# Second attention: where TensorE issues the products of the weighted values, and the order of the score banks

## The reference

```python
qk = jnp.einsum('bhdq,bhdl->bhql', qh, kh) * scale      # qh, kh: 32 sequences, 8 heads, 8 x 256
sm = jax.nn.softmax(qk, axis=-1)
ret = jnp.einsum('bhql,bhdl->bhdq', sm, vh)
return gamma * ret.reshape(B, Dv, Lq)
```

## Time and profile before

| | |
|---|---|
| median of 3 runs | 675.91 us (674.12 to 676.22) |
| the profiled execution's own time | 673.21 us |
| its span, first to last instruction | 671.5 us |
| mean granted TensorE clock | 0.952 of full speed |
| PE busy | 603.9 us, 90% of the span |
| DVE busy | 489.4 us, 73% |
| ACT busy | 404.1 us, 60% |
| POOL busy | 313.0 us, 47% |

### The profile page before, as it was taken

How to read it: one execution, slowest core, us unless ns; L and a number is a source line. 1 busy time by engine, 2 the same in 40 slices (tenths; PEclk the granted TensorE clock), 3 DMA queues, 4 the chain that set the end, 5 groups by cost and what they waited for, 6 DMA issues and landing times. The chain is left out here.

```text
span 671.5 us, 16680 instructions
## 1 busy us (share of the span) xinstructions
PE 603.9 (90%) x4997; PEld 460.1 (69%) x4997; DVE 489.4 (73%) x999; ACT 404.1 (60%) x829; POOL 313.0 (47%) x430
## 2 busy tenths in 40 slices
PE   3688877999999966999999999999789699999995
PEld 2577765788888865655555555555478599999884
DVE  2877886788978796598899999996556634444756
ACT  3888884344434441488898888998645145555431
POOL 2455555023222557934675765753237334024254
PEclk9989997999999987699999999999969889999998
DMA  5434438400000014344444444440002435446344
GB/s 163 114 99 130 130 105 290 155 1 1 0 0 1 23 50 137 106 132 130 129 145 127 138 139 123 143 139 29 2 1 75 130 102 187 145 150 189 109 141 127
DMA packets 72601, 71.20 MB, mean 106 GB/s; under 512 B 12364, under 2 KB 68812, under 8 KB 72556
## 3 DMA queue, kind: packets, MB, share of 16 engines
q1 hardware_dynamic: 67324, 56.33, 28.2%
q0 software_dynamic: 5232, 14.29, 6.9%
HBM read 38.48 MB, written 31.36 MB: 104 GB/s over the span
## 5 line engine op out<-in xcount | busy, mean ns | idle before, releaser
L1420 DVE TENSOR_REDUCE a_smax<-a_s 128x2 f32<-128x512 f32 x256 | 164.7, 681 | 19.9 <-PE a_s L1348 15.1
L1242 ACT ACTIVATE a_prob<-a_st 128x512 f32<-128x512 f32 x256 | 141.8, 597 | 23.8 <-PE a_st L1343 22.7
L1348 PE MATMUL a_s<-kop,qop 64*128 64x256 f32 x512 | 106.3, 324 | 5.6 <-DVE a_smax L1420 3.4
L1343 PEld LDWEIGHTS a_st<-qop,kop 64*128 64x128 f32 x512 | 70.8, 187 | 56.8 <-issue 24.9
L1343 PE MATMUL a_st<-qop,kop 64*128 64x256 f32 x512 | 104.0, 315 | 0.6 <-DVE a_smax L1420 0.5
L1303 PE MATMUL a_pv<-a_prob,a_vt 128*32 128x256 f32 x1024 | 81.6, 391 | 3.2 <-ACT a_pv_sb L1227 1.7
L819 POOL TENSOR_TENSOR f_hs_lo<-f_kept,f_hs_hi 128x512 fp32r<-128x512 f32 x32 | 41.3, 1320 | 85.5 <-ACT f_hs_hi L769 85.5
L1348 PEld LDWEIGHTS a_s<-kop,qop 64*128 64x128 f32 x512 | 73.0, 193 | 7.9 <-DVE a_smax L1420 4.8
L1871 POOL DMA_INDIRECT sorted_rows<-m_xn,m_slot x32 | 33.5, 1047 | 46.1 <-PE m_gu L128 26.6
L126 PE MATMUL f_bank<-f_xt_hi,w_hi 128*128 128x512 f32 x128 | 51.2, 400 | 1.1 <-DVE w_raw L865 0.6
L127 PE MATMUL f_bank<-f_xt_lo,w_hi 128*128 128x512 f32 x128 | 50.5, 395 | 0.0
(11 more groups left out here) (263 smaller groups left out, 1663.4 us busy)
## 6 DMA issues: line engine op xcount, KB each, us to landing
qop<-qop_rows SPq DMA_DIRECT2D x64, 100.0 KB
kop<-kop_rows SPq DMA_DIRECT2D x64, 96.0 KB
sorted_rows<-x_all SPq DMA_DIRECT2D x2, 2944.0 KB, 15.4
qop<-sorted_rows SPq DMA_DIRECT2D x46, 128.0 KB, 2.3
expert_rows<-turned SPq DMA_DIRECT2D x46, 128.0 KB
kop_rows<-k_hi SPq DMA_DIRECT2D x32, 128.0 KB, 2.3
qop_rows<-q_hi POOLq DMA_DIRECT2D x30, 128.0 KB, 2.7
x_all<-in_x SPq DMA_DIRECT2D x4, 512.0 KB, 5.8
```

What stands on the lines that cost most here:

```text
L1242: act.activation(prob[:, u % 8], st_ps[BANK[u]][:], ACT.Exp, scale=SCALE1).then_inc(prob_ready, 1)
L1343: st = pe.matmul(st_ps[BANK[u]][:, c * D:(c + 1) * D], lhsT=kop[t.slot][rows, u // 2, c * P:(c + 1) * P], rhs=qop[t.slot][rows, u // 2], s ...
L1348: sm = pe.matmul(s_ps[BANK[u]][:, c * D:(c + 1) * D], lhsT=qop[v.slot][rows, w // 2, c * P:(c + 1) * P], rhs=kop[v.slot][rows, w // 2], st ...
L1420: dve.tensor_reduce(smax[:, v.slot, opposite(u)], s_ps[BANK[u]][:].rearrange("p (q n) -> p q n", q=2), AX_X, ALU.max).then_inc(smax_ready, 1)
```

## The change

In `attention1` alone, two edits. The products of a quad are now issued with both halves together, at u = 2 (quad 3 of the tile before), 6 (quad 0), 10 (quad 1) and 14 (quad 2), so that the score matmuls of four units stand in a row between them: units 15, 0, 1, 2; then 3 to 6; 7 to 10; 11 to 14. Both calls of `selected` stand behind the products at u = 6, and the turn that stood behind unit 11 stands behind the products of u = 10. The turn at u = 2 stays there and comes ahead of the products; the transposes of the values stay at u = 14, behind the products.

The banks turn in another order at the tile's end: units 13, 14, 15 take banks 2, 1, 2 in place of 1, 2, 1. So unit 13 follows unit 11 in its bank, where before unit 1 followed unit 15.

```diff
-        BANK = [u % 3 for u in range(UNITS - 1)] + [1]
+        BANK = [u % 3 for u in range(UNITS - 3)] + [2, 1, 2]
...
-                    if u in (1, 3):
-                        products(o, 3, u // 2)
-                    if u % 2 and u > 3:
-                        products(t, u // 4 - 1, u % 4 // 2)
-                    if u in (5, 7):
-                        selected(p, (u - 5) // 2)
-                    if u == 11:
+                    if u % 4 == 2:
+                        for c in range(DC):
+                            products(t if u > 4 else o, (u // 4 + 3) % QUADS, c)
+                    if u == 6:
+                        for m in range(2):
+                            selected(p, m)
+                    if u == 10:
                         def before():
                             after(pe, neg_t_ready, t, 2)
                             after(pe, back_ready, p)
```

## The result

| | median | lowest to highest | runs |
|---|---|---|---|
| before | 675.47 us | 674.12 to 676.22 | 4 |
| changed | 689.70 us | 687.75 to 690.26 | 4 |

The ratio is 1.0208, with a 95% interval of 1.0181 to 1.0234: the change costs 14.2 us. 688.5 was forecast, in a range of 680 to 697.

What follows compares the result with a forecast made beforehand. PE's own row was taken to set the 12.47 us step; the change's chain of waits on DVE makes it 13.31, 0.84 more. Over 15 steps 12.6 us, added to 675.91, give 688.5 us, range 680 to 697.

Steps and rivals of the forecast that it cites:

- What bounds the kernel before: Second attention: PE's own row sets the step, 12.36 of 12.47 us counted, with DVE following at about 11.2.
- What the change takes away: PE leaves the scores at four places instead of nine; its own work falls 1.68 us per step to 10.47.
- The chain that it adds: Each group's fourth unit waits for DVE's first reduce; four groups sum to 13.31 us, 0.84 more per step.
- The release: Time from the end of a group's first reduce to PE's next weight load: 0.11 us, bounds 0.05 to 0.14.
- The wait of unit 0: Rival: the maxima's transfer reaches unit 0 late; at 0.3 us more per step, 693 us; chance 0.04.
- the maxima's transfer alone holds unit 0: The copy behind unit 11 starts the transfer unit 0 waits for, at least 2.1 us left; 2.27 was enough.
- The two cancel: Rival: no change, each group 0.2 us shorter and the step 12.5 us; chance 0.07.
- The saved switches: Rival: three banks cover the gaps, DVE sets the step at 11.2 us, about 657 us; chance 0.07.
- The clock did fall: Rival: PE's idle pieces lower its clock, 0.5 to 2.1 us more per step, 696 to 720 us; chance 0.05.
- a clock below 1.00 between 290 and 460 us: Sign in the second attention's trace that would show the forecast wrong.
- The argument that made this rival small: PE's new busy share, 10.5 of 13.3, lies between stage start (clock 0.50) and end (10.60 of 12, 1.00), nearer the end.
- The turn of the banks costs nothing by itself: With the old bank order unit 1 would wait for unit 15 likewise; the 0.24 us only falls into that group.

Runs made afterwards that it cites:

- e9_quarter_loads: The changed kernel with operands of the next tile's units 0 to 7 loaded in two parts, units 0 to 3 already once unit 3 is used; 684.6 us.
- e4_threes: The kernel before with score units in groups of three, both halves of a quad's products together, fewer breaks, another bank order and ACT's copies moved; 679.0 us.

## Why the prediction was right, and where it was not

- **What bounds the kernel before: right.** PE's own row. With DVE's and ACT's work cut, most of its steps moved by at most 0.07 us.
- **What the change takes away: right in size.** Sixteen records and the way back took 364.22 - 363.22 = 1.00, products and both calls of `selected` 361.47 - 359.60 = 1.87 (1.88). The four score groups lost their breaks as counted.
- **The chain that it adds: right in kind, one term too large.** The release was 0.05 us, the lower bound named, and not 0.11: 4 x 0.06 = 0.24 per step, 13.31 - 0.24 = 13.07 against 13.10 measured. Group by group, 3.68, 3.11, 3.41 and 3.11 were forecast, and 3.62, 3.06, 3.36 and 3.06 measured in e9_quarter_loads. Over 15 steps the term was 3.2 us too high. The row it rested on the earlier trace rows has unit 1 waiting for DVE and ACT at once, so it does not say whose release it shows.
- **The wait of unit 0: under-weighted.** It was a rival at 0.04, priced at 0.3 per step on top. It came, with 0.5 per step on average (13.62 against 13.12), over half of it in one step, and with 4.4 to 5.1 us of time. Its cause was also placed wrongly: the step that failed is the sentence that the maxima's transfer alone holds unit 0. That transfer by itself was in time: in e9_quarter_loads 2.39 us were enough for it (2.27 in the earlier trace rows). What had to be watched are the operand loads in SP's queue, which start at unit 7. Before, they had 6.7 to 6.9 us until unit 0; the change left 6.2, in a step that is longer.
- **The two cancel in part.** 12.6 us were forecast, all of it for the chain; 14.2 were measured, 9.8 for the chain and 4.4 for unit 0. The median lies 1.2 us from the forecast, which is better than the terms are: that is luck.
- **The rivals.** The saved switches don't come through, since every gap is longer than three banks cover. The clock did fall once: the sign named for it, a clock below 1.00 between 290 and 460 us, is there from 413 to 418 us. But it came behind the wait of 2.84 us and cost 1.1 us; through the groups' short waits (0.34 to 0.8 us, PE busy 10.17 of 12) it was 1.00, as it was between 290 and 460 us of every other run's trace. The argument that made this rival small was misread: 10.5 of 13.3 is 0.79, nearer to the first row (8.91 of 12, 0.74) than to the second (0.88). What the Trainium skill (TensorE: Matmul & The Clock Gate, A second HAM failure mode: psum-queue depth-cycling) tells of brief idle times between groups that cycle banks does not show in these runs.
- **The turn of the banks costs nothing by itself:** right for the undisturbed step, 13.10 with either order.

## What to carry to other kernels

A row of producer work that is one unit longer than the number of buffers puts the consumer's first unit, its release and the whole gap on one chain, and then each microsecond of each gap counts; keep the rows no longer than the buffers, and see that two units that share a buffer at a short distance have a block between them. Here rows that fit only brought the time back to that of before (0.996 to 1.000), not below it. Before moving blocks, write down the distance from the event that lets a load start to the first use of its data, and compare it with what the load has now: when it shrinks to what was just enough, the wait appears, and the trace may name another releaser for it. And work saved on the engine that sets the pace is only worth what the next limit leaves: here 1.7 us per step were saved on PE and 0.7 lost.

## What had not been expected of the hardware

The time from the end of a consumer to PE's next matmul differs by how it is waited for: 0.05 us behind DVE's reduce (359.12 to 359.17), 0.13 behind ACT's exponential (404.80 to 404.93). It is not the engine alone: in e4_threes PE went on 0.05 behind ACT's copy (364.96 to 365.01). In the program the wait for that copy is the last one ahead of the products, as the wait for DVE is the last one ahead of a unit, while the wait for the exponential stands earlier in the row of waits. That this order makes the difference was not tried.

And one wait of 2.84 us was followed by three microseconds at half the clock, 1.1 us of loss on top of the wait, while the short waits of the groups, 0.34 to 0.58 us, left it at 1.00.
